# Score products on halves of the array's rows, and the row maxima's offset on VectorE, in a fused image-token transformer layer

## The reference, cut to what matters

```python
attn = jnp.einsum('bhnd,bhmd->bhnm', q, k) * Dh ** (-0.5)   # 12 heads, Dh = 16
attn = fq_act(attn, s_attn)                                  # integers of 8 bits
x_int = x_int - jnp.max(x_int, axis=-1, keepdims=True)       # row maximum
x_int = jnp.maximum(x_int, n * x0_int)                       # the clamp
q = jnp.floor(x_int / x0_int)
...
out = jnp.exp2(-jnp.clip(big, 0.0, qmax - 1.0))              # powers of two
o = jnp.einsum('bhnm,bhmd->bhnd', attn, v)
```

## Time and profile before

| | us |
|---|---|
| median of 3 runs | 3518.93 (3518.01 to 3521.01) |
| the profiled execution, its own time | 3518.62 |
| its span, first to last instruction | 3516.8 |
| mean granted TensorE clock | 0.989 of full speed |

### The profile page before, as it was taken

How to read it: one execution, slowest core, us unless ns; L and a number is a source line. 1 busy time by engine, 2 the same in 40 slices (tenths; PEclk the granted TensorE clock), 3 DMA queues, 4 the chain that set the end, 5 groups by cost and what they waited for, 6 DMA issues and landing times.

```text
span 3516.8 us, 98077 instructions
## 1 busy us (share of the span) xinstructions
PE 3381.6 (96%) x30764; PEld 2898.6 (82%) x30764; DVE 3368.5 (96%) x10279; ACT 3153.6 (90%) x6228; POOL 806.2 (23%) x1647
## 2 busy tenths in 40 slices
PE   1589999999999999999999999999999999999999
PEld 1368888888888888888888888888888888888888
DVE  6699999999999999999999999999999999999995
ACT  2799999999999999999999999999999999999992
POOL 3222222222222222222221221222222222222210
PEclk9789999999999999999999999999999999999999
DMA  5101001000000000000000110100000000000000
GB/s 125 27 14 25 25 16 26 25 20 23 25 20 23 24 22 21 24 23 20 25 24 18 25 25 16 26 25 17 25 25 20 23 25 21 22 24 23 20 10 8
DMA packets 157123, 85.77 MB, mean 24 GB/s; under 512 B 51451, under 2 KB 154370, under 8 KB 156610
## 3 DMA queue, kind: packets, MB, share of 16 engines
q1 hardware_dynamic: 153692, 78.82, 9.0%
q10 hardware_dynamic: 2918, 0.67, 0.1%
HBM read 54.89 MB, written 12.24 MB: 19 GB/s over the span
## 4 chain that ended last, share of the span: by engine, by line
PE 92%; DVE 1%; issue 1%; ACT 0%; POOLq 0%; DVEq 0%; POOL 0%
PE pU L1183 33%; PE pY L1209 20%; PE pX L1075 5%; PE pX L1132 5%; PE pS L1120 4%; PE pS L1111 4%; PE pS L1121 4%; PE pX L1094 3%; PE pW L1195 3%; PE pO L1142 2%; PE pY L1192 1%; PE pX L1102 1%; PE pX L1088 1%; PE pX L1151 1%; PE pX L1082 1%
## 5 line engine op out<-in xcount | busy, mean ns | idle before, releaser
L1183 PE MATMUL pU<-x2T,UG 128*128 128x250 f16 x8704 | 1231.6, 270 | 1.0 <-ACT work L676 0.9
L1183 PEld LDWEIGHTS pU<-x2T,UG 128*128 128x128 f16 x8704 | 823.0, 97 | 108.7 <-ACT work L676 1.5
L1209 PE MATMUL pY<-WD,work 128*128 128x192 f32 (+1 forms) x4352 | 810.0, 328 | 0.0
L1209 PEld LDWEIGHTS pY<-WD,work 128*128 128x128 f32 (+1 forms) x4352 | 690.8, 187 | 3.9
L962 DVE SCALAR_TENSOR_TENSOR work<-work,cst 128x249 f32<-128x249 f32 (+1 forms) x1536 | 658.6, 484 | 8.4 <-issue 4.3
L623 ACT ACTIVATE work<-work,alpha 128x249 f32<-128x249 f32 (+1 forms) x1536 | 648.3, 509 | 15.2 <-DVE alpha L974 14.0
L607 ACT ACTIVATE work<-a,room 128x249 bf16<-128x249 int8 (+1 forms) x1536 | 648.3, 514 | 0.0
L1183 PE MATMUL pU<-x2T,UGB 67*128 67x250 f16 x2176 | 592.4, 272 | 0.0
L942 DVE TENSOR_REDUCE rmax<-a 128x4 f32<-128x996 int8 (+1 forms) x384 | 452.9, 1179 | 40.9 <-ACT a L598 40.9
L632 ACT ACTIVATE passing<-pX,cst 128x512 int16<-128x512 int16 (+3 forms) x768 | 480.8, 687 | 6.9 <-PE pX L1132 3.5
L598 ACT ACTIVATE a<-pS,cst 128x996 int8<-128x996 f32 (+1 forms) x384 | 421.4, 1097 | 70.3 <-PE pS L1111 70.1
(11 more groups left out here) (209 smaller groups left out, 5337.5 us busy)
## 6 DMA issues: line engine op xcount, KB each, us to landing
img<-in_x_dram SPq DMA_DIRECT2D x896, 23.5 KB
img<-in_x_dram SPq DMA_DIRECT2D x768, 21.4 KB
qz<-qb SPq DMA_DIRECT2D x768, 15.6 KB, 1.8
h<-in_txt_dram SPq DMA_DIRECT2D x64, 96.0 KB, 2.0
out_dram<-yout SPq DMA_DIRECT2D x64, 96.0 KB
out_dram<-yout SPq DMA_DIRECT2D x64, 90.8 KB
WD<-in_L_ffn_Wd_dram SPq DMA_DIRECT2D x1, 1536.0 KB, 7.6
work<-in_L_ffn_Wu_dram SPq DMA_DIRECT2D x2, 512.0 KB, 6.6
```

The lines of the kernel that those rows point to most:

```text
L1183: a = mm(pU[:, s, q * EVEN:(q + 1) * EVEN], weights, x2T[i % 2][0:w, m, 0:EVEN], start=m == 0, stop=m == BLOCKS - 1)
L1209: a = mm(pY[0:n, t * 256:t * 256 + D], (act_[k % 2] if k else up[0])[:, c:c + n], WD[:, e, :], start=k == 0 and t == 0, stop=e == E - 1, s ...
```

## The change

It does three things. `score` uses only the 64 rows of the array in which its head lies: heads 0 and 1 the lower half, 2 and 3 the upper, in the order 0, 2, 1, 3, so that neighbours use different halves and write to different banks. `peak` is issued on VectorE instead of GpSimd, with the same arithmetic and the same two waits. `ORDER` is replaced by another permutation of the same 254 stages; its shifts run from 0 to -4 instead of 0 to -5, since the step is cut at another place of the cycle (from `embed` to `result` lie about four steps in both). The new list is shown whole.

```diff
         ORDER = [
-            ("r_score", -4, -1), ("low", -3, 4), ("mmG", -5, 7), ("r_biased", -4, -1), ("weigh", -3, 3),
-            ("qkq", -2, 5), ("turnp", -3, 3), ("alpha", -3, 5), ("conv", -2, 2), ("r_pairs", -4, -1),
-            ("down", -5, 5), ("top", -2, 0), ("act", -5, 6), ("gate", -5, 7), ("grow", -3, 4),
...
+            ("gate", -4, 3), ("square", -2, 2), ("below", -2, 4), ("lmax", -3, -1), ("turn", -1, 0),
+            ("copy", -1, 0), ("square", -2, 3), ("down", -4, 2), ("turn", -1, 1), ("copy", -1, 1),
+            ("mmU", -4, 4), ("expo", -2, 2), ("below_max", -3, -1), ("quot", -2, 4), ("qk", -1, 0),
+            ("gates", -3, -1), ("low", -2, 1), ("sum", -2, 2), ("u", -2, 4), ("qk", -1, 1), ("r_ratio", -3, -1),
+            ("peak", -2, 5), ("silu", -4, 4), ("vconv", -2, -1), ("mmG", -4, 4), ("weigh", -2, 0),
+            ("mmU", -4, 5), ("qkq", -1, 0), ("act", -4, 3), ("below", -2, 5), ("grow", -2, 1), ("qkq", -1, 1),
+            ("square", -2, 4), ("qk", -1, 2), ("down", -4, 3), ("r_exp", -3, -1), ("turnp", -2, 0),
+            ("power", -2, 3), ("r_sum", -3, -1), ("alpha", -2, 2), ("silu", -4, 5), ("qkq", -1, 2),
+            ("quot", -2, 5), ("r_inverse", -3, -1), ("pick", -4, 4), ("share", -2, 2), ("gate", -4, 4),
+            ("expo", -2, 3), ("power", -2, 4), ("mmU", -4, 6), ("sum", -2, 3), ("power", -2, 5),
+            ("r_score", -3, -1), ("act", -4, 4), ("copyp", -2, 0), ("weigh", -2, 1), ("silu", -4, 6),
+            ("mmG", -4, 5), ("qk", -1, 3), ("qkq", -1, 3), ("conv", -1, 0), ("low", -2, 2), ("u", -2, 5),
+            ("pick", -4, 5), ("r_biased", -3, -1), ("turnp", -2, 1), ("square", -2, 5), ("expo", -2, 4),
+            ("mmU", -4, 7), ("alpha", -2, 3), ("copyp", -2, 1), ("gate", -4, 5), ("grow", -2, 2),
+            ("mmG", -4, 6), ("qk", -1, 4), ("r_pairs", -3, -1), ("share", -2, 3), ("qzload", -1, 0),
+            ("silu", -4, 7), ("sum", -2, 4), ("act", -4, 5), ("r_top_pairs", -3, -1), ("weigh", -2, 2),
+            ("down", -4, 4), ("qkq", -1, 4), ("conv", -1, 1), ("gate", -4, 6), ("r_take_pairs", -3, -1),
+            ("alpha", -2, 4), ("expo", -2, 5), ("share", -2, 4), ("low", -2, 3), ("mmG", -4, 7),
+            ("pick", -4, 6), ("act", -4, 6), ("qk", -1, 5), ("qkq", -1, 5), ("value", -2, 0), ("score", -1, 0),
+            ("value", -2, 1), ("mmU", -4, 8), ("turnp", -2, 2), ("qzload", -1, 1), ("quant", -1, 0),
+            ("grow", -2, 3), ("top", -1, 0), ("gate", -4, 7), ("peak", -1, 0), ("sum", -2, 5), ("conv", -1, 2),
+            ("low", -2, 4), ("alpha", -2, 5), ("pick", -4, 7), ("score", -1, 1), ("down", -4, 5),
+            ("mmG", -4, 8), ("outq", -2, 0), ("weigh", -2, 3), ("silu", -4, 8), ("turnp", -2, 3),
+            ("copyp", -2, 2), ("r_penalty", -3, -1), ("act", -4, 7), ("down", -4, 6), ("score", -1, 2),
+            ("grow", -2, 4), ("quant", -1, 1), ("share", -2, 5), ("pick", -4, 8), ("value", -2, 2),
+            ("copyp", -2, 3), ("low", -2, 5), ("gate", -4, 8), ("weigh", -2, 4), ("down", -4, 7),
+            ("top", -1, 1), ("r_masked", -3, -1), ("mmU", -3, 0), ("below", -1, 0), ("quant", -1, 2),
+            ("silu", -3, 0), ("quot", -1, 0), ("mmG", -3, 0), ("turnp", -2, 4), ("r_top", -3, -1),
+            ("value", -2, 3), ("grow", -2, 5), ("outcast", -2, 0), ("u", -1, 0), ("r_take", -3, -1),
+            ("mmU", -3, 1), ("imgload", 0, -1), ("qzload", -1, 2), ("weigh", -2, 5), ("r_weight", -3, -1),
+            ("copyp", -2, 4), ("act", -4, 8), ("outq", -2, 1), ("turnp", -2, 5), ("outcast", -2, 1),
+            ("top", -1, 2), ("square", -1, 0), ("peak", -1, 1), ("r_part0", -3, -1), ("down", -4, 8),
+            ("copyp", -2, 5), ("value", -2, 4), ("power", -1, 0), ("value", -2, 5), ("r_rest", -3, -1),
+            ("v", -1, -1), ("below", -1, 1), ("gate", -3, 0), ("score", -1, 3), ("r_part1", -3, -1),
+            ("expo", -1, 0), ("outq", -2, 2), ("vq", -1, -1), ("mmG", -3, 1), ("peak", -1, 2),
+            ("result", -4, -1), ("quot", -1, 1), ("sum", -1, 0), ("silu", -3, 1), ("gate", -3, 1),
+            ("outcast", -2, 2), ("project", -2, -1), ("prq", -2, -1), ("u", -1, 1), ("r_part2", -3, -1),
+            ("residual", -2, -1), ("power", -1, 1), ("stats2", -2, -1), ("mmU", -3, 2), ("quant", -1, 3),
+            ("chosen", -3, -1), ("down", -3, 0), ("top", -1, 3), ("mean2", -2, -1), ("below", -1, 2),
+            ("square", -1, 1), ("spread2", -2, -1), ("quot", -1, 2), ("peak", -1, 3), ("score", -1, 4),
+            ("copyw", -3, -1), ("expo", -1, 1), ("embed", 0, -1), ("quant", -1, 4), ("score", -1, 5),
+            ("norm2", -2, -1), ("pick", -3, 1), ("below", -1, 3), ("sum", -1, 1), ("alpha", -1, 0),
+            ("split2", -2, -1), ("quot", -1, 3), ("top", -1, 4), ("silu", -3, 2), ("embed_h", 0, -1),
+            ("act", -3, 1), ("txtload", 0, -1), ("mmG", -3, 2), ("mmU", -3, 3), ("pick", -3, 2),
+            ("turn2", -2, 0), ("share", -1, 0), ("down", -3, 1), ("stats", 0, -1), ("gate", -3, 2),
+            ("quant", -1, 5), ("silu", -3, 3), ("turn2", -2, 1), ("alpha", -1, 1), ("mean", 0, -1),
+            ("spread", 0, -1), ("peak", -1, 4), ("u", -1, 2), ("act", -3, 2), ("power", -1, 2), ("pick", -3, 3),
+            ("low", -1, 0), ("norm", 0, -1), ("copy2", -2, 0), ("top", -1, 5), ("share", -1, 1),
+            ("store", -4, -1), ("copy2", -2, 1), ("split", 0, -1), ("grow", -1, 0), ("mmG", -3, 3),
+            ("route", -2, -1), ("logit", -2, -1), ("u", -1, 3),
...
@@ -509,12 +509,6 @@
                         wait(pv_done, UNITS * i)
                         nc_.tensor_scalar(vb[:, :, :, 0:DH], v8[:].rearrange("p t (h d) -> p t h d", d=DH),
                                           V_LIFT, 0.0, ALU.mult, ALU.add).then_inc(v_done, 1)
-                    elif stage == "peak":
-                        n, b = NTOK[k % 2], k % 2
-                        wait(mx_done, UNITS * i + k + 1)
-                        wait(bl_done, UNITS * i + k - 1)
-                        nc_.tensor_scalar(room[b][0:n, :], rmax[b][0:n, :], -1.0, cc(C_L, n), ALU.mult,
-                                          ALU.add).then_inc(pk_done, 1)
                     elif stage == "outcast":
                         wait(o_q, GROUPS * i + k + 1)
                         wait(pj_ps, i)
@@ -987,6 +981,12 @@
                         after(dve, prT_ps, UNITS * i + k - 1)
                         ts(prob[b][0:n, :], grown[b][0:n, :].bitcast(I16), EXPONENT, None,
                            ALU.bitwise_and).then_inc(pr_done, 1)
+                    elif stage == "peak":
+                        n, b = NTOK[k % 2], k % 2
+                        dve.wait_ge(mx_done, UNITS * i + k + 1)
+                        after(dve, bl_done, UNITS * i + k - 1)
+                        ts(room[b][0:n, :], rmax[b][0:n, :], -1.0, cc(C_L, n), ALU.mult,
+                           ALU.add).then_inc(pk_done, 1)
                     elif stage == "prq":
                         dve.wait_ge(pj_ps, i + 1)
                         after(dve, h2_done, i)
@@ -1107,9 +1107,10 @@
                         n, g, t = NTOK[k % 2], k // 2, k % 2
                         pe.wait_ge(qz_in[g], 16 * PER * (i + 1))
                         take_s(a_done, UNITS * i + k + 1)
-                        for m in range(PER):
+                        for m in (0, 2, 1, 3):
+                            rows = slice(m // 2 * 2 * QUAD, (m // 2 + 1) * 2 * QUAD)
                             a = mm(pS[0:n, m // 2, (m % 2) * TOKENS:(m % 2 + 1) * TOKENS],
-                                   qz[:, g * PER + m, tcols[t]], kb[:, g, :], start=True, stop=True)
+                                   qz[rows, g * PER + m, tcols[t]], kb[rows, g, :], start=True, stop=True)
                         a.then_inc(s_ps, 1)
                     elif stage == "u":
                         n, b = NTOK[k % 2], k % 2
```

More of the change, by code:

```diff
@@ L310, in fused_layer @@
-            ("below", -2, 0), ("mmG", -5, 8), ("weigh", -3, 4), ("value", -3, 3), ("low", -3, 5),
-            ("act", -5, 7), ("grow", -3, 5), ("top", -2, 1), ("turnp", -3, 4), ("down", -5, 6),
-            ("r_take_pairs", -4, -1), ("gate", -5, 8), ("r_penalty", -4, -1), ("weigh", -3, 5), ("pick", -5, 8),
-            ("outq", -3, 1), ("r_masked", -4, -1), ("act", -5, 8), ("copyp", -3, 4), ("outcast", -3, 1),
-            ("score", -2, 2), ("down", -5, 7), ("value", -3, 4), ("quant", -2, 2), ("quot", -2, 0),
@@ L315, in fused_layer @@
-            ("mmU", -4, 0), ("top", -2, 2), ("peak", -2, 1), ("r_top", -4, -1), ("below", -2, 1),
-            ("turnp", -3, 5), ("power", -2, 0), ("score", -2, 3), ("down", -5, 8), ("r_take", -4, -1),
-            ("quot", -2, 1), ("mmG", -4, 0), ("copyp", -3, 5), ("value", -3, 5), ("result", -5, -1),
-            ("power", -2, 1), ("quant", -2, 3), ("outq", -3, 2), ("qzload", -2, 2), ("v", -2, -1),
-            ("silu", -4, 0), ("vq", -2, -1), ("u", -2, 0), ("outcast", -3, 2), ("r_weight", -4, -1),
@@ L320, in fused_layer @@
```

(21 more changed lines are left out.)

17 lines of the change are left out of this document (removed).

## The result

The changed kernel takes 3547.57 us (median of 3 runs, 3546.81 to 3547.61), against 3518.93 before: ratio 1.008, 95% interval 1.0057 to 1.0102. It is 28.6 us slower, where 12 us less were forecast. The time lies just above the range's upper end (3546), which was the price of the third rival, "DVE becomes the bound, slower". The experiments show that its number was close and its reason was not.

What follows compares the result with a forecast made beforehand. PE was taken to set the pace, with DVE 1% behind. PE at 51.83 and DVE at 51.74 to 52.08 us an image gave 51.94, 0.19 less; over 64 images 12 us, so 3507 us, range 3484 to 3546.

Steps and rivals of the forecast that it cites:

- DVE becomes the bound, slower: DVE keeps 0.9 us of waits an image at other places and `peak` adds 0.42: 3546 us; chance 0.15.
- A `score` stage alone gains nothing: On PE, 0.09 way in, 0.21 for two turns and 0.13 way out make 0.43 us, as before.
- The rival that took the speedup alone: On PE, up to 2x for 64 rows without the cost of mode changes; DVE's floor then gives 3491 us; chance 0.13.
- PE gives back 0.30: PE an image: 1.28 us less from halves, 0.88 more for eight mode changes, 0.1 more for exposed weight loads.
- `peak` costs 6 x 0.07: Six `peak` instructions moved to DVE add 0.07 us each, 0.42 an image; upper bound 0.16 each.
- The list takes DVE's four losses away: On DVE, the new order removes losses an image at `vq` (0.34 us), `mean2` (0.24), `lmax` (0.12) and `r_part2` (0.11).
- PE 51.83 with the small waits it has now: PE's time an image after the change, 0.3 us less, from 51.7 to 52.0, with its present waits kept.
- SP's loads are covered: The image's 26 transfers hold SP 9.6 us, but SP reaches them 10 us earlier, so PE's `embed` doesn't wait.
- Filling and emptying within 3 us: Pipeline ends stay as they are, to within 3 us, since `embed` to `result` stays about four steps.
- 52.13 us an image: The old kernel's pace, read from the same instruction's return one image on; 64 times that is 3336 us.
- 51.94: Forecast pace in us an image, from PE 51.83 and DVE 51.74 to 52.08; 0.19 less than before.
- The first rival: Row mode changes cost little, DVE's 51.74 us sets the pace: some 0.43 less an image, 3491 us; chance 0.13.

## Why the prediction was wrong

**The pace by starts.** For each line of PE the table has the mean time from a start to the next start on the engine, per image, all instructions from 500 to 3200 us, in us.

| PE, what is multiplied | before | new list and `peak` | after |
|---|---|---|---|
| `score` | 2.68 | 2.67 | 2.03 |
| `down` (f32) | 11.39 | 11.54 | 11.85 |
| `embed` (f32) | 3.34 | 3.42 | 3.62 |
| `pick` | 1.74 | 1.82 | 1.92 |
| `u`, second half | 2.61 | 2.86 | 2.87 |
| `route` and `project` (last lines) | 0.42 | 0.76 | 0.77 |
| `mmU`, `mmG`, last block | 4.26 | 3.89 | 3.90 |
| distance of an image | 52.23 | 52.84 | 52.92 |

**Step by step.**
- *A `score` stage alone gains nothing*: right, 0.41 to 0.45 against 0.43. Rows cost what columns do, as read from the setup. With the Trainium skill's rule ("TensorEngine Tiling (Array Packing)", Key Properties), that a change of mode drains TensorE, these traces agree: 0.09 us is lost on the way in, and 0.10 to 0.14 on the way out. The rival that took the speedup alone is excluded.
- *PE gives back 0.30*: it didn't. The 0.30 holds two things. `value` 4 and 5 side by side save two changes, 0.22, and that belongs to the list. The halves alone are then ten changes more in the new list, and the same working has them give back 0.08. Measured (last two columns), they cost 0.08, so the working is off by 0.16 there and by 0.10 in the old list. `score` gives back 0.64, and `down` takes 0.31, `embed` 0.20, `pick` 0.10 and `v` 0.09 of it. Changes cost 0.10 each and loads some 0.1 an image, about what the prediction had. What it lacked is the f32 stage behind a change: its 0.11 was read next to f16 and bf16 products. Such a stage is longer by 0.10, at two places in either list. `down` takes 1.40 from 2040.51 to 2041.91, where one without a change takes 1.30.
- *`peak` costs 6 x 0.07*: mis-sized: 0.13 at four places, 0.04 at one, and 0.45 at one, with the wait. The row of line 969 has no operand from a tile; this one has. The upper bound, 0.16, held it. It weighs little: with the immediate 3.7 us come back.
- *The list takes DVE's four losses away*: it does. `v` ahead of `vq` no longer waits (11.9 us in the stretch from 1000 to 3000 us before, 0.2 after), and `mean2`, `lmax` and `r_part2` lost their gaps. But new ones came: `act` 1 behind `embed_h` 0.19, `act` 2 behind `peak` 4 0.25. And the excess of DVE's longer instructions, those that lie over one of POOL, went from 0.24 us an image to 0.76.
- *"PE 51.83 with the small waits it has now"*: this is the step that failed. The prediction looked for what the new list does to DVE, and took over PE's waits as they were: PE's distance became 52.92. Of the 1.09 between, 0.10 is the base, 52.13 for 52.23, and 0.16 the halves; 0.83 is the list, which was to give PE 0.22 and took 0.61 (52.23 to 52.84, with `peak` on DVE). The middle column, without halves, shows 0.25 more behind `u` and 0.34 more behind `route` and `project`, less 0.37 behind `mmU` and `mmG`, of which 0.23 was an old wait for `copyw`. The waits view of the changed kernel, 1000 to 2000 us, has two of them at the weight loads:

```profile
PEld pX L1094 <- issue: 9.7, 19, 0.5
PEld pX L1082 <- POOL xs L528: 7.9, 19, 0.4
```

`qk` 1 stands one product behind `qk` 0 and needs its bank back from ACT; `turn` 0 waits for POOL's `split`. The two largest sums of the table, behind `route` and behind `project`, are waits of the next `u` for ACT, which has to empty `pS` (line 592 is `quant`, line 608 `square`). ACT's timeline, then PE's:

```profile
2002.22 1.10 ACT L592 ACTIVATE a<-pS,cst 121x996 int8<-121x996 f32 x1
...
2016.93 1.08 ACT L608 ACTIVATE work<-pS,cst 128x996 f32<-128x996 f32 x1
...
2022.61 0.56 ACT L637 ACTIVATE qk<-pX,qk_bias,qk_scale 128x249 int8<-128x249 f32 x1
```

```profile
2003.46 0.39 PE L1121 MATMUL pS<-work,ident 121*121 121x498 bf16 x1
...
2018.16 0.39 PE L1121 MATMUL pS<-work,ident 121*121 121x498 bf16 x1
...
2023.31 0.48 PE L1094 MATMUL pX<-xT,wT 128*128 128x249 f16 x3
```

Each of the three starts 0.14 or 0.15 us after ACT's end (2003.32, 2018.01, 2023.17). None of this is seen if only DVE's queue is compared. By starts the new kernel's PE has 0.78 us of waits an image: 0.16 and 0.18 for the two `u`, 0.13 for `turn` 0, 0.22 for `qk` 1, and 0.09 ahead of `project`. The old one has 0.32: 0.22 for `copyw` and 0.10 ahead of `project`. Without them PE takes 52.1, against 51.9, so two thirds of the 0.69 are waits.

- *SP's loads are covered*: right, `embed` waits for no transfer. *Filling and emptying within 3 us*: wrong, 15 us less; the prediction counted the distance from `embed` to `result` alone. It comes with the list: from the last `embed` to the end the old list takes 168.7 us, and 168.8 with halves; the new list alone takes 164.4, and 163.2 with `peak` on DVE.
- *52.13 us an image*: one distance of two that alternate. The mean over fifty is 52.23. The forecast is a difference, so this moved it by nothing, but the 51.83 and 51.94 stand 0.10 too low. The first rival's "some 0.43 less" is 0.39 by its own 51.74.

**The rival that came nearest.** "DVE becomes the bound, slower" was priced at 3546. That the time came out 1.6 us beside it is luck. It expected 0.9 us of waits on DVE and 0.42 on top, and DVE is busy 99.3% in the steady stretch. Had the study stopped at the profile, this would have been the story. Shortening DVE by 1.05 us an image gives back 4.6 us of 28.6, lengthening PE costs 84% of what is put in. Without its waits PE takes 52.1 us an image and DVE 52.4, and the pace is 52.9: neither engine's work alone makes it. That it is the waits on both, each for the other and for ACT and POOL, is what the traces say. The runs show that the list carries the loss; no run takes PE's new waits away and nothing else.

What stays open: which single entry of the new list costs most. Two entries were moved, in one kernel, and it got worse. The places of the two `u` that wait for ACT were not moved, and neither was `conv`, whose instructions lie over DVE's longer ones. How the 51 us of the list alone divide was not tried. The fastest version measured is the old kernel with three entries moved, 3505.07 us, 0.4% below the old one; its combination with immediates in `quot` was not run.

## What to carry to other kernels

When two engines are each within 1% of the pace, a new order has to be checked for both: go through each engine's own queue and ask for every entry which bank or tile it needs back, and from whom. A filler in front of a waiting instruction is worth more than its duration; moved one place it cost 73 us here. A wait that is seen can be the harmless end of a ring, and to remove it by delaying the waiter passes it on: `act` 1, put later in order to take a wait off DVE, made PE wait 0.50 us for its bank. And make sure which stage a line of the timeline is, by its neighbours in the list, before moving it. And to name the bound, lengthen and shorten each engine by a known amount instead of reading its busy share.
